# Taking the last 464 nodes of a graph layer as two groups of 232 instead of 384 and 80

## The chip, the cores and the metric

The kernel runs on one core of a Trainium2 chip. The metric is the time of one execution on the device in microseconds (us), lower is better, given as the median of several runs. The profile records one more execution of the same program.

## What is computed

A layer of a graph network with a residual and a layer norm, in float32, on 50,000 nodes of 128 features and 25,000 edges that are sorted by their target:

```
msg = relu(x[src] + edge_attr)            # 25000 x 128
agg = segment_sum(msg, dst, 50000)        # sum of the messages of each target node
h   = x + agg
h   = relu(relu(h @ W1 + b1) @ W2 + b2)   # 128 -> 256 -> 128
out = layernorm(x + h)                    # over the 128 features, no gain or bias
```

## The kernel before

**Groups and tiles.** The nodes are taken in groups of G = 384, three tiles (T = 3) of 128 nodes. Node `g*384 + 3*p + t` lies on partition p in tile t, so that the load or store of a group is one DMA with 128 partitions of 1,536 contiguous bytes. 50,000 nodes are 130 groups of 384 and one of 80 (LP = 80 partitions, LT = 1 tile). The last group has number 130 (`LAST`), the one before it 129 (`END`).

**Edges.** A group takes its messages from K = 2 chunks of 128 edges. Where a group's first chunk starts is found on the chip (`prepare`), from the sorted targets, and flags are set where the chunks would not hold all edges of a group; a slow general path stands behind them for such inputs. For each chunk `select` (L616) makes a matrix of zeros and ones, edge by node column, and the messages are multiplied with it on TensorE. An ordinary group's chunk reaches only 72 columns of each tile (WP), from column 0 or from column 56 (LO). The chunks of END reach 72 and 96 columns (END_WP), those of LAST all of its 80; LAST takes only one chunk, the last 128 edges.

**The steps of one group,** each with its engine:
- SyncE (SP) issues the load of x (`start_x`, L122), of the edge attributes (`start_edge_attr`, L126) and the store of the result (`store`, L552). GpSimd (POOL) issues the gathers x[src], one for each chunk (`start_gather`, L132).
- VectorE (DVE) adds the gathered rows to the edge attributes (`add_edge_attr`, L639). ScalarE (ACT) takes the relu as msg_hi (`high_part`, L809), and DVE the remainder msg_lo (`low_part`, L651).
- TensorE (PE) turns x into hT_ps (`turn_x` L906, or within `sum_turned` L934) and adds the messages there (`sum_messages` L916): hi and lo part of each chunk. ACT copies the sum (`copy_hT`, L815).
- PE makes the two halves of the hidden layer (`hidden_sum`, L973), ACT their relu (`hidden`, L821), PE the output (`output_sum`, L985).
- DVE adds b2 (`add_bias`, L658; for LAST a matmul with a row of ones does that, `bias_sum` L98), takes the relu and adds x (`add_x`, L674), and makes the statistics (`statistics` L686, `aggregate` L693). ACT makes the standard deviation (`deviation`, L827), DVE its reciprocal and the shift (`reciprocal` L702, `shifts` L707).
- The normalized result y is written by ACT (`normalize`, L837; tiles 0 and 1 of a group) and POOL (`third_tile`, L586; tile 2).

**What sets the order.** Each engine works through a list that is written out by hand (`main_sync`, `main_gpsimd`, `main_vector`, `main_scalar`, `main_tensor`), and semaphores hold an engine until its inputs are there. PE runs `hidden_sum(g)`, then the sum of the messages of g+1, then `output_sum(g)`. Loads are issued five groups ahead, gathers four.

**The end.** The last four groups have their tiles shared out one by one: POOL takes tiles 0 and 1 of group 127 and tiles 1 and 2 of END (L607), ACT tile 2 of group 127, all three of group 128 and tile 0 of END (L893 to L903), DVE the one tile of LAST (`normal_tile`, L713). The lines of the DVE's end are these:

```python
        add_x(LAST)
        statistics(LAST)
        reciprocal(END)
        shifts(END)
        aggregate(LAST)
        reciprocal(LAST)
        shifts(LAST)
        normal_tile(LAST, 0).then_inc(last_y_ready, 1)
```

SP then issues the store of END (L563) and of LAST (L583), 192 KB and 40 KB, and waits until all stores have landed.

Of the kernel before, what the change touches and what calls it, by code (L numbers as in the profile page):

```python
# [5 lines left out]
FP32R = mybir.dt.float32r  # L6
# [18 lines left out]
WP = 72  # L25
END_LO, END_WP = 32, 96
BOUNDS = [0, T * SPLIT, G]


FIRST_ROW = 2  # L30
LP, LT = 80, 1

# [21 lines left out]


def partitions(g, c):
    return LP if g == c["LAST"] else 128


def tiles(g, c):  # L60
    return LT if g == c["LAST"] else T


def windows(g, c):
    return 1 if g == c["LAST"] else K


def parts(g, c):

    return PARTS.get(g, [slice(0, windows(g, c))])  # L70

# [11 lines left out]
def gathers_to(slot, g, c):  # L83

    return 16 * sum(windows(i, c) for i in range(slot, g + 1, EB) if i >= FIRST_GROUPS)

# [39 lines left out]
def start_edge_attr(sp, edge_attr, g, first, c):  # L126
    n = windows(g, c)
    sp.dma_start(c["pre_msg"][:, g % EB, 0:n, :],
                 edge_attr[bass.ds(first, n * EW), :].rearrange("(k p) d -> p k d", p=EW)).then_inc(c["ea_loaded"][g % EB], 16)


def start_gather(nc, x, g, k, loaded, c):  # L132
    index = c["last_pairs"][:, 0:1] if g == c["LAST"] else c["src_of"][:, g - FIRST_ROW, k:k + 1]
# [28 lines left out]
def target_nodes(nc, dve, dst_ps, c):  # L162
    R = c["R"]
    base = c["node_row"][:, 0, :]
    dve.wait_ge(c["dst_T_ready"], 1)
    nc.vector.tensor_tensor(c["dst_of"][:, :, 0], dst_ps[:, 0, :], base, ALU.subtract)
    nc.vector.scalar_tensor_tensor(c["dst_of"][:, 0:R - 1, 1], dst_ps[:, 1, 0:R - 1], -float(T * LO[1]), base[:, 0:R - 1],
                                   ALU.add, ALU.subtract)
    return nc.vector.scalar_tensor_tensor(c["dst_of"][:, R - 1:R, 1], dst_ps[:, 1, R - 1:R], -float(T * END_LO), base[:, R - 1:R],
                                          ALU.add, ALU.subtract)  # L170
# [11 lines left out]
def prepare(nc, x, edge_attr, dst, pairs, w1, b1, w2, b2, c, sb, sem):  # L182
# [89 lines left out]
    def prepare_gpsimd(pool):  # L272
# [30 lines left out]
                       channel_multiplier=0, allow_small_or_imprecise_dtypes=True).then_inc(pool_consts, 1)  # L303
        nc.gpsimd.iota(c["node_in_last"][:, :], pattern=[[1, LP]], base=0,
                       channel_multiplier=0, allow_small_or_imprecise_dtypes=True).then_inc(pool_consts, 1)

# [87 lines left out]
    def prepare_vector(dve):  # L394
# [13 lines left out]
        for k in range(1, K + 1):  # L408
            last = nc.vector.tensor_scalar(node_row[:, k, :], node_row[:, k, :], float(BOUNDS[k]), None, ALU.add)
        link(dve, last)  # L410
        dve.wait_ge(pool_consts, 3)
        for k in range(1, K + 1):
            last = nc.vector.tensor_scalar(range_node[:, k:k + 1], range_node[:, k:k + 1], float(BOUNDS[k]), None, ALU.add)
        link(dve, last)
        nc.vector.tensor_scalar(least[:, :], range_node[:, K:K + 1], c["LAST"] * G - 0.5, float(edges - 2 * EW), ALU.is_gt, ALU.mult)

# [60 lines left out]
def main_path(nc, x, pairs, edge_attr, out, c, sb, sem, checks):  # L477
# [18 lines left out]

    x_src, sel, end_sel, last_sel = c["x_src"], c["sel"], c["end_sel"], c["last_sel"]
    msg_hi = sb("msg_hi", [128, EB, K, D], FP32R)
# [41 lines left out]
    def main_sync(sp):  # L540
# [5 lines left out]
        def load_ea(g):  # L546
            first = c["EDGES"] - EW if g == LAST else window_start_of(nc, g, c)
            if g >= EB:
                sp.wait_ge(msg_lo_ready, parts_to(g - EB + 1, c))
            start_edge_attr(sp, edge_attr, g, first, c)  # L550

        def store(g):  # L552
            if g < LAST - 3:
                sp.wait_ge(y_ready, g + 1)
                if g >= POOL_FROM:
                    sp.wait_ge(y_tile_ready, g - POOL_FROM + 1)
            elif g == LAST - 3:
                sp.wait_ge(y_pool_ready, 1)
            elif g == END:
                sp.wait_ge(y_pool_ready, 2)  # L560
            if g >= LAST - 3:
# [20 lines left out]
        sp.wait_ge(last_y_ready, 1)  # L582
        sp.dma_start(rows(out, LAST, c), y[0:LP, LAST % YB, 0:LT, :]).then_inc(out_stored[LAST % YB], 16)  # L583

    def main_gpsimd(pool):
# [8 lines left out]
        for g in range(FIRST_GROUPS, GROUPS):  # L594
# [3 lines left out]
            if g == LAST:  # L598
                pool.wait_ge(c["last_pairs_loaded"], 16)
            for k in range(windows(g, c)):  # L600
                start_gather(nc, x, g, k, xsrc_loaded[g % EB], c)
# [4 lines left out]

        for g, ts in ((LAST - 3, (0, 1)), (END, (1, 2))):  # L607
            pool.wait_ge(shift_ready, g + 1)
            pool.wait_ge(out_stored[g % YB], (g // YB) * 16)
            for t in ts:  # L610
                last = nc.gpsimd.tensor_scalar(y[:, g % YB, t, :], z[:, g % ZB, t, :], rstd[:, g % SB, t:t + 1],
                                               shift[:, g % SB, t:t + 1], ALU.mult, ALU.add)
# [190 lines left out]
    def main_scalar(act):  # L803
# [66 lines left out]
        for g in range(3, LAST):  # L870
# [6 lines left out]
            for t in range(T):  # L877
# [4 lines left out]
                if t == 0 and g == LAST_DST_AT:  # L882
                    act.wait_ge(c["last_pairs_loaded"], 16)
                    nc.scalar.activation(c["last_dst"][:, :], c["last_pairs"][:, 1:2], ACT.Copy).then_inc(last_dst_ready, 1)
                if t == 0 and g == END:
# [11 lines left out]
        normalize(LAST - 2, 0)  # L897
        normalize(LAST - 2, 1)
        normalize(LAST - 2, 2).then_inc(y_act_ready, 1)
        deviation(END)  # L900
        deviation(LAST)
        y_free(END)
        normalize(END, 0).then_inc(y_act_ready, 1)  # L903

    def main_tensor(pe):
# [10 lines left out]
        def sum_messages(g):  # L916

            n = tiles(g, c)
            pe.wait_ge(msg_lo_ready, parts_to(g, c) + 1)
            for k in range(windows(g, c)):  # L920
                if g == LAST:
                    p0, p1, tile = 0, LP, last_sel[:, :]
                elif g == END:
                    p0, p1 = (0, WP) if k == 0 else (END_LO, END_LO + END_WP)
                    tile = end_sel[:, k, :]
                else:
                    p0, p1, tile = LO[k], LO[k] + WP, sel[:, g % EB, k, :]
                cols = tile.rearrange("p (t q) -> p t q", t=n)[:, :, 0:p1 - p0]
                for part in (msg_hi, msg_lo):
                    last = nc.tensor.matmul(sum_bank(g)[:, 0:n, p0:p1], part[:, g % EB, k, :], cols,  # L930
                                            start=False, stop=(k == windows(g, c) - 1), skip_group_check=True)
            last.then_inc(hT_summed, 1)
# [331 lines left out]
def gnn_resnorm_kernel(nc, x, dst, pairs, edge_attr, w1, b1, w2, b2, out, h_dram):  # L1264
# [4 lines left out]
    GROUPS = -(-nodes // G)  # L1269
    assert D == 128 and HC * 128 == hidden and nodes == (GROUPS - 1) * G + LP * LT  # L1270
    R = GROUPS - 1 - FIRST_ROW

    ctx = ExitStack()
    with ctx:
# [6 lines left out]
        def sem(name):  # L1281
# [13 lines left out]
            node_in_range=sb("node_in_range", [128, 1, T * WP]),  # L1295
            node_in_last=sb("node_in_last", [128, LP]),
# [4 lines left out]
            last_pairs=sb("last_pairs", [EW, 2], INT32),  # L1301
            last_dst=sb("last_dst", [EW, 1]),
            last_pairs_loaded=sem("last_pairs_loaded"),
            end_sel=sb("end_sel", [EW, K, T * END_WP], FP32R),
            last_sel=sb("last_sel", [EW, LP], FP32R),
            first_sel=sb("first_sel", [EW, len(FIRST_SELS), T * 128], FP32R),
# [109 lines left out]
```

## Time and profile before

| | |
|---|---|
| median of 3 runs | 462.42 us (461.7 to 462.5) |
| the profiled execution: its time | 461.7 us |
| its span in the profile | 460.0 us |
| mean granted TensorE clock | 0.997 |
| PE, DVE, ACT, POOL busy | 98%, 94%, 86%, 80% |
| moved by DMA | 86.8 MB, 189 GB/s |

The time is what a run reports; the span is what the profiler recorded between the first and the last event of the same execution. A matmul on float32 is two records in the profile, so two matmuls stand there as x4. The ends of PE's records are modelled, so the distance from start to start says more than the duration. Names are those of the program with numbers left out: `h_ps` is h2_ps0 and h2_ps1, `w_sb` w1_sb and w2_sb, and so on. SPq is the queue in which SP issues DMAs. In a view of the DMA the line "DMA" gives the busy share of the 16 engines in tenths, in 40 equal slices of the stretch; "under 512 B" counts the small packets among all; a queue's line gives packets, MB, and the time that its packets took as a share of the 16 engines' time.

### The profile page before, as it was taken

The numbers are of one execution on the slowest core, as the hardware profiler recorded it, in microseconds if no ns is written. First come the engines' busy times: TensorE is split into PE (matmuls) and PEld (weight loads), VectorE is DVE, ScalarE is ACT, GpSimd is POOL, SyncE is SP. The second block draws the span as 40 slices with busy tenths as digits, with TensorE's granted clock in tenths as the row PEclk, the third lists the DMA queues.
The fourth block names the chain that finished last, engine by engine and source line by source line (L and its number), as shares of the span: only waits on it lengthen the run. The fifth ranks groups of instructions, "written<-read, shape, count | busy, mean of one in ns | idle before, by whom it ended". The sixth has DMA issues, their size and how long they took to land.

```text
span 460.0 us, 10662 instructions
## 1 busy us (share of the span) xinstructions
PE 451.1 (98%) x3033; PEld 379.3 (82%) x3033; DVE 433.6 (94%) x1759; ACT 394.2 (86%) x928; POOL 369.8 (80%) x403
## 2 busy tenths in 40 slices
PE   7999999999999999999999999999999999999995
PEld 6788888888888888888888888888888888888884
DVE  6799999999999999999999999999999999999996
ACT  3599888888888888988988888888888888888886
POOL 7777888888888888768888888888888888888842
PEclk9999999999999999999999999999999999999998
DMA  5576666666666666666666666666666666666632
GB/s 135 150 224 196 197 202 192 197 190 195 204 185 201 191 195 201 182 195 200 193 206 182 200 199 195 184 198 199 200 195 191 194 200 198 194 199 189 200 113 89
DMA packets 83870, 86.82 MB, mean 189 GB/s; under 512 B 12023, under 2 KB 79508, under 8 KB 83812
## 3 DMA queue, kind: packets, MB, share of 16 engines
q1 hardware_dynamic: 75044, 68.77, 48.0%
q0 software_dynamic: 8496, 17.38, 13.9%
q8 instruction: 24, 0.39, 0.4%
q14 instruction: 34, 0.28, 0.2%
q10 hardware_dynamic: 272, 0.00, 0.0%
HBM read 60.51 MB, written 25.60 MB: 187 GB/s over the span
## 4 chain that ended last, share of the span: by engine, by line
PE 95%; DMA 2%; DVE 1%; ACT 1%; issue 0%; DVEq 0%
PE h_ps L990 38%; PE h1T_ps L982 36%; PE hT_ps L942 11%; PE hT_ps L937 9%; DMA x_src<-in_x_dram,first_pairs 1%; DMA window<-in_pairs_dram,window_start_i 1%; DMA pre_msg<-in_edge_attr_dram 1%; DMA first_pairs<-in_pairs_dram 0%; DVE stats L690 0%; PE hT_ps L913 0%; PE hT_ps L930 0%; DVE pre_msg L648 0%; DVE z L683 0%; DVE before_in_row L321 0%; ACT std L830 0%
## 5 line engine op out<-in xcount | busy, mean ns | idle before, releaser
L134 POOL DMA_INDIRECT x_src<-in_x_dram,src_of x254 | 270.2, 1064 | 67.5 <-issue 59.8
L990 PE MATMUL h_ps<-w_sb,h1T 128*128 128x128 f32 x1564 | 198.0, 276 | 0.0
L982 PE MATMUL h1T_ps<-hT,w_sb 128*128 128x384 f32 (+1 forms) x524 | 190.2, 486 | 0.5 <-ACT hT L819 0.5
L990 PEld LDWEIGHTS h_ps<-w_sb,h1T 128*128 128x128 f32 x1564 | 185.3, 192 | 0.3 <-ACT h1T L825 0.2
L825 ACT ACTIVATE h1T<-h1T_ps,b_sb 128x384 f32<-128x384 f32 (+1 forms) x262 | 151.3, 578 | 37.6 <-PE h1T_ps L982 29.3
L982 PEld LDWEIGHTS h1T_ps<-hT,w_sb 128*128 128x128 f32 x524 | 89.5, 191 | 35.2 <-ACT hT L819 0.7
L844 ACT ACTIVATE y<-z,shift,rstd 128x128 f32<-128x128 f32 x263 | 114.6, 483 | 1.1 <-DVE shift L710 0.4
L590 POOL TENSOR_SCALAR y<-z,rstd,shift 128x128 f32<-128x128 f32 x123 | 87.4, 711 | 13.5 <-DVE shift L710 9.0
L942 PE MATMUL hT_ps<-sel,msg_hi 128*128 128x216 f32 x250 | 94.8, 447 | 0.0
L690 DVE BATCH_NORM_STATS2 stats<-z 128x6 f32<-128x128 f32 x391 | 88.6, 282 | 0.1
L937 PE MATMUL hT_ps<-ident,x_sb 128*128 128x128 f32 x375 | 87.6, 273 | 0.0
L664 DVE TENSOR_TENSOR h<-h_ps,b_sb 128x384 f32<-128x384 f32 x130 | 72.3, 556 | 15.1 <-PE h_ps L990 2.1
L631 DVE TENSOR_TENSOR sel<-node_in_range,dst_of 128x432 fp32r<-128x432 f32 x126 | 76.0, 603 | 0.0
L683 DVE SCALAR_TENSOR_TENSOR z<-h,x_sb 128x384 f32<-128x384 f32 x130 | 71.8, 552 | 0.0
L942 PE MATMUL hT_ps<-sel,msg_lo 128*128 128x216 f32 x250 | 70.1, 348 | 0.0
L813 ACT ACTIVATE msg_hi<-pre_msg 128x256 fp32r<-128x256 f32 (+1 forms) x134 | 55.0, 411 | 15.0 <-DVE pre_msg L648 10.2
L819 ACT ACTIVATE hT<-hT_ps 128x384 f32<-128x384 f32 (+1 forms) x130 | 63.5, 488 | 3.3 <-PE hT_ps L968 2.4
L937 PEld LDWEIGHTS hT_ps<-ident,x_sb 128*128 128x128 f32 x375 | 53.0, 141 | 15.1
L942 PEld LDWEIGHTS hT_ps<-sel,msg_hi 128*128 128x128 f32 x250 | 47.4, 190 | 18.3 <-issue 3.9
L648 DVE TENSOR_TENSOR pre_msg<-pre_msg,x_src 128x256 f32<-128x256 f32 (+1 forms) x134 | 57.9, 432 | 3.2 <-DMA x_src<-in_x_dram,first_pairs 1.6
L655 DVE SCALAR_TENSOR_TENSOR msg_lo<-pre_msg,msg_hi 128x256 fp32r<-128x256 f32 (+1 forms) x134 | 55.1, 411 | 2.6 <-ACT msg_hi L813 1.2
L942 PEld LDWEIGHTS hT_ps<-sel,msg_lo 128*128 128x128 f32 x250 | 47.5, 190 | 0.1
(120 smaller groups left out, 183.3 us busy)
## 6 DMA issues: line engine op xcount, KB each, us to landing
x_sb<-in_x_dram SPq DMA_DIRECT2D x130, 192.0 KB, 2.5
out_dram<-y SPq DMA_DIRECT2D x130, 192.0 KB
pre_msg<-in_edge_attr_dram SPq DMA_DIRECT2D x130, 128.0 KB, 2.8
x_src<-in_x_dram,src_of POOLq DMA_INDIRECT x254, 3.0
w_sb<-in_w_dram SPq DMA_DIRECT2D x2, 128.0 KB, 2.6
dst_rows<-in_dst_dram SPq DMA_DIRECT2D x1, 97.7 KB
x_src<-in_x_dram,first_pairs POOLq DMA_INDIRECT x6, 2.8
b_sb<-in_b_dram SPq DMA_DIRECT2D x1, 64.0 KB, 3.2
```

The costliest lines, as they stand in the source:

```text
L134: nc.gpsimd.indirect_dma_start(out=c["x_src"][:, g % EB, k, :], out_offset=None, in_=x, in_offset=bass.IndirectOffsetOnAxis(ap=index, axis ...
L590: nc.gpsimd.tensor_scalar(y[:, g % YB, 2, :], z[:, g % ZB, 2, :], rstd[:, g % SB, 2:3], shift[:, g % SB, 2:3], ALU.mult, ALU.add).then_inc ...
L631: nc.vector.tensor_tensor(sel[:, g % EB, :, :], node_in_range[:, :, :].to_broadcast([128, K, T * WP]), dst_of[:, g - FIRST_ROW:g - FIRST_R ...
L664: nc.vector.tensor_tensor(h2[0:p, g % 2, 0:n, :], h2_ps[g % 2][0:p, 0:n, :], b2_sb[0:p, :, :].to_broadcast([p, n, D]), ALU.add).then_inc(h ...
L683: nc.vector.scalar_tensor_tensor(z[0:p, g % ZB, 0:n, :], h2_of[0:p, 0:n, :], 0.0, x_sb[0:p, g % XB, 0:n, :], ALU.max, ALU.add).then_inc(z_ ...
L690: last = nc.vector.bn_stats(stats[0:p, g % SB, t, :], z[0:p, g % ZB, t, :])
L825: nc.scalar.activation(h1T[:, h, 0:n, 0:p], h1T_ps[h][:, 0:n, 0:p], ACT.Relu, bias=b1_sb[:, h:h + 1]).then_inc(h1_ready, 1)
L844: return nc.scalar.activation(y[0:p, g % YB, t, :], z[0:p, g % ZB, t, :], ACT.Identity, bias=shift[0:p, g % SB, t:t + 1], scale=rstd[0:p, ...
L937: nc.tensor.matmul(hT_ps[:, t, :], x_sb[:, g % XB, t, :], ident[:, :], is_transpose=True, start=False, stop=False, skip_group_check=True)
L942: return nc.tensor.matmul(hT_ps[:, 0:T, LO[k]:LO[k] + WP], part[:, g % EB, k, :], cols, start=start, stop=stop, skip_group_check=True)
L982: nc.tensor.matmul(h1T_ps[h][:, 0:n, 0:p], w1_sb[:, h * 128:(h + 1) * 128], hT[:, 0:n, 0:p], start=True, stop=True).then_inc(h1_summed, 1)
L990: last = nc.tensor.matmul(h2_ps[g % 2][0:p, t, :], h1T[:, h, t, 0:p], w2_sb[:, h, :], start=(h == 0 and t == 0 and not biased(g, c)), stop ...
```

## The change

The number of groups stays 131. The groups 129 (END) and 130 (LAST) become halves of the last 464 nodes: 116 partitions (HALF_P) and two tiles (HALF_T), 232 nodes each. Both take two chunks of edges, and every chunk's matrix reaches all 232 columns (`half_sel`, `node_in_half` take the place of `end_sel`, `last_sel`, `node_in_last`). The chunks of LAST are the last 256 edges. The bounds that `prepare` looks for are capped at the first node of LAST. The tiles at the end are shared out anew: POOL takes tiles 0 and 1 of group 127, tile 2 of group 128 and tile 1 of END; ACT tile 2 of 127, tiles 0 and 1 of 128, tile 0 of END and tile 1 of LAST; DVE tile 0 of LAST. The core of the diff:

```diff
-END_LO, END_WP = 32, 96
-LP, LT = 80, 1
+HALF_P, HALF_T = 116, 2
+HALF = HALF_P * HALF_T
...
+def half(g, c):
+    return g >= c["LAST"] - 1
 def partitions(g, c):
-    return LP if g == c["LAST"] else 128
+    return HALF_P if half(g, c) else 128
 def tiles(g, c):
-    return LT if g == c["LAST"] else T
+    return HALF_T if half(g, c) else T
+def first_node(g, c):
+    return (c["LAST"] - 1) * G + HALF if g == c["LAST"] else g * G
...
 def rows(dram, g, c):
-    t = tiles(g, c)
-    return dram[g * G:g * G + partitions(g, c) * t, :].rearrange("(p t) d -> p t d", t=t)
+    t, n0 = tiles(g, c), first_node(g, c)
+    return dram[n0:n0 + partitions(g, c) * t, :].rearrange("(p t) d -> p t d", t=t)
...
-            sp.dma_start(rows(out, g, c), y[:, g % YB, :, :]).then_inc(out_stored[g % YB], 16)
+            sp.dma_start(rows(out, g, c), y[0:partitions(g, c), g % YB, 0:tiles(g, c), :]).then_inc(out_stored[g % YB], 16)
...
-        sp.dma_start(c["last_pairs"][:, :], pairs[c["EDGES"] - EW:c["EDGES"], :]).then_inc(c["last_pairs_loaded"], 16)
+        sp.dma_start(c["last_pairs"][:, :, :], pairs[c["EDGES"] - K * EW:c["EDGES"], :].rearrange("(k p) a -> p k a", p=EW),
+                     allow_slow_non_contiguous=True).then_inc(c["last_pairs_loaded"], 16)
...
         sp.wait_ge(last_y_ready, 1)
-        sp.dma_start(rows(out, LAST, c), y[0:LP, LAST % YB, 0:LT, :]).then_inc(out_stored[LAST % YB], 16)
+        sp.wait_ge(y_act_ready, 4)
+        sp.dma_start(rows(out, LAST, c), y[0:HALF_P, LAST % YB, 0:HALF_T, :]).then_inc(out_stored[LAST % YB], 16)
...
-        for g, ts in ((LAST - 3, (0, 1)), (END, (1, 2))):
+        for g, ts in ((LAST - 3, (0, 1)), (LAST - 2, (2,)), (END, (1,))):
...
-                for k, width in ((0, WP), (1, END_WP)):
-                    last = nc.vector.tensor_scalar(
-                        end_sel[:, k, :].rearrange("p (t q) -> p t q", t=T)[:, :, 0:width],
-                        c["node_in_group"][:, :].rearrange("p (t q) -> p t q", t=T)[:, :, 0:width],
-                        dst_of[:, g - FIRST_ROW, k:k + 1], None, ALU.is_equal)
-                last.then_inc(sel_ready, 1)
+                nc.vector.tensor_tensor(half_sel[:, 0, :, :], c["node_in_half"][:, :, :].to_broadcast([128, K, HALF]),
+                                        dst_of[:, g - FIRST_ROW:g - FIRST_ROW + 1, :].rearrange("p a k -> p k a").to_broadcast([128, K, HALF]),
+                                        ALU.is_equal).then_inc(sel_ready, 1)
...
-                nc.vector.tensor_scalar(last_sel[:, :], c["node_in_last"][:, :], c["last_dst"][:, 0:1], -float(LAST * G),
-                                        ALU.subtract, ALU.is_equal).then_inc(sel_ready, 1)
+                for k in range(K):
+                    last = nc.vector.tensor_scalar(half_sel[:, 1, k, :], c["node_in_half"][:, 0, :], c["last_dst"][:, k:k + 1],
+                                                   -float(first_node(LAST, c)), ALU.subtract, ALU.is_equal)
+                last.then_inc(sel_ready, 1)
...
         normalize(LAST - 2, 0)
-        normalize(LAST - 2, 1)
-        normalize(LAST - 2, 2).then_inc(y_act_ready, 1)
+        normalize(LAST - 2, 1).then_inc(y_act_ready, 1)
         deviation(END)
-        deviation(LAST)
         y_free(END)
         normalize(END, 0).then_inc(y_act_ready, 1)
+        deviation(LAST)
+        act.wait_ge(shift_ready, LAST + 1)
+        y_free(LAST)
+        normalize(LAST, 1).then_inc(y_act_ready, 1)
```

How the lists of the engines change is shown at two places.

The end of ScalarE's list before, from the hidden layer of LAST on (std is a `deviation`, y a `normalize`):

```order
L825 ACTIVATE h1T<-h1T_ps1,b1_sb 128x80 [waits h1_summed]
L844 ACTIVATE y<-z,shift,rstd 128x128 [waits shift_ready,out_stored1]
L844 ACTIVATE y<-z,shift,rstd 128x128 [waits shift_ready,out_stored2]
L844 ACTIVATE y<-z,shift,rstd 128x128 x2
L830 ACTIVATE std<-mean_var,eps_col 128x3 [waits var_ready]
L830 ACTIVATE std<-mean_var,eps_col 80x1 [waits var_ready]
L844 ACTIVATE y<-z,shift,rstd 128x128 [waits shift_ready,out_stored3]
```

The same with the change:

```order
L832 ACTIVATE h1T<-h1T_ps1,b1_sb 128x2x116 [waits h1_summed]
L851 ACTIVATE y<-z,shift,rstd 128x128 [waits shift_ready,out_stored1]
L851 ACTIVATE y<-z,shift,rstd 128x128 [waits shift_ready,out_stored2]
L851 ACTIVATE y<-z,shift,rstd 128x128
L837 ACTIVATE std<-mean_var,eps_col 116x2 [waits var_ready]
L851 ACTIVATE y<-z,shift,rstd 116x128 [waits shift_ready,out_stored3]
L837 ACTIVATE std<-mean_var,eps_col 116x2 [waits var_ready]
L851 ACTIVATE y<-z,shift,rstd 116x128 [waits out_stored4,shift_ready]
```

One `normalize` of group 128 has left the list, the one of END now stands ahead of the `deviation` of LAST, and a `normalize` of LAST has come at the end.

The end of SyncE's list before, the last loads and the stores:

```order
L563 DMA out_dram<-y 128x384 [waits y_tile_ready,y_ready]
L123 DMA x_sb<-in_x_dram 80x128 [waits z_ready]
L128 DMA pre_msg<-in_edge_attr_dram 128x128 [waits msg_lo_ready]
L563 DMA out_dram<-y 128x384 [waits y_tile_ready,y_ready] x6
L563 DMA out_dram<-y 128x384 [waits y_act_ready,y_pool_ready]
L563 DMA out_dram<-y 128x384 [waits y_act_ready]
L563 DMA out_dram<-y 128x384 [waits y_act_ready,y_pool_ready]
L583 DMA out_dram<-y 80x128 [waits last_y_ready]
```

The same with the change:

```order
L568 DMA out_dram<-y 128x384 [waits y_tile_ready,y_ready]
L129 DMA x_sb<-in_x_dram 116x256 [waits z_ready]
L133 DMA pre_msg<-in_edge_attr_dram 128x2x128 [waits msg_lo_ready]
L568 DMA out_dram<-y 128x384 [waits y_tile_ready,y_ready] x6
L568 DMA out_dram<-y 128x384 [waits y_act_ready,y_pool_ready] x2
L568 DMA out_dram<-y 116x256 [waits y_act_ready,y_pool_ready]
L590 DMA out_dram<-y 116x256 [waits y_act_ready,last_y_ready]
```

The count of DMAs is the same; the last two stores have 116 partitions of 1,024 bytes each, in place of 128 partitions of 1,536 and 80 of 512.

## Rows read from the trace of the kernel before

**Rows 1.** The page: span, and the chain that ended last.

```profile
span 460.0 us, 10662 instructions
...
PE 95%; DMA 2%; DVE 1%; ACT 1%; issue 0%; DVEq 0%
```

**Rows 2.** Timeline of PE, 449 to 453 us: start, duration, line, operation.

```profile
451.00 0.28 PE L930 MATMUL hT_ps<-last_sel,msg_hi 128*128 128x80 f32 x1
...
451.22 1.58 PE L990 MATMUL h_ps<-w_sb,h1T 128*128 128x128 f32 x12
452.64 0.57 PE L982 MATMUL h1T_ps<-hT,w_sb 128*128 128x80 f32 x4
```

**Rows 3.** Chain that ended last, in order of time, 452 to 460 us.

```profile
452.44 0.19 ACT std L830
...
452.87 0.21 DVE shift L710
453.07 0.48 DVE h L664
...
453.57 0.57 DVE z L683
...
454.17 0.69 DVE stats L690 x3
...
454.98 0.31 DVE mean_var L699 x3
...
455.50 0.29 DVE stats L690
...
455.90 0.17 DVE shift L710
...
456.18 0.30 ACT std L830
...
456.89 0.34 DVE y L717
```

**Rows 4.** Timeline of all engines, 455.9 to 457.6 us.

```profile
456.16 0.88 POOL L611 TENSOR_SCALAR y<-z,rstd,shift 128x128 f32<-128x128 f32 x2 [2.67 <-DVE shift L710]
...
456.38 0.48 ACT L844 ACTIVATE y<-z,shift,rstd 128x128 f32<-128x128 f32 x1
...
457.06 0.33 SPq L563 DMA_DIRECT2D out_dram<-y  x1
...
457.45 0.42 SPq L583 DMA_DIRECT2D out_dram<-y  x1
```

**Rows 5.** DMA, 457.2 to 460 us: the stores of END and LAST.

```profile
DMA  0000000000799999997762000000000000000000
...
DMA packets 240, 0.24 MB, mean 85 GB/s; under 512 B 32, under 2 KB 240, under 8 KB 240
```

**Rows 6.** DMA, 455.9 to 456.8 us: the store of group 128 alone.

```profile
DMA packets 144, 0.20 MB, mean 219 GB/s; under 512 B 16, under 2 KB 144, under 8 KB 144
...
q1 hardware_dynamic: 144, 0.20, 60.0%
```

**Rows 7.** DMA, 0 to 3 us: the first loads of the targets.

```profile
DMA packets 558, 0.02 MB, mean 8 GB/s; under 512 B 530, under 2 KB 558, under 8 KB 558
...
q10 hardware_dynamic: 272, 0.00, 4.8%
```

**Rows 8.** DMA, 2.9 to 3.2 us: the load of dst_rows alone.

```profile
q1 hardware_dynamic: 29, 0.02, 26.1%
```

**Rows 9.** Groups by line and form, 440 to 460 us: busy us, mean ns, idle.

```profile
L655 DVE SCALAR_TENSOR_TENSOR msg_lo<-pre_msg,msg_hi 128x256 fp32r<-128x256 f32 x3 | 1.3, 418 | 0.0
...
L683 DVE SCALAR_TENSOR_TENSOR z<-h_ps,x_sb 80x128 f32<-80x128 f32 x1 | 0.3, 254 | 0.0
```

**Rows 10.** Timeline of SP and POOL, 437 to 441 us: last load of x, last gather.

```profile
437.68 0.33 SPq L123 DMA_DIRECT2D x_sb<-in_x_dram  x1
...
439.43 0.98 POOL L134 DMA_INDIRECT x_src<-in_x_dram,last_pairs  x1 [0.17 <-issue]
```

More of the change, by code:

```diff
@@ L53 @@
 FLAGS = 7 + FIRST_CHUNKS + UPPER_CHUNKS
+def half(g, c):
+    return g >= c["LAST"] - 1
 def partitions(g, c):
-    return LP if g == c["LAST"] else 128
+    return HALF_P if half(g, c) else 128
 def tiles(g, c):
-    return LT if g == c["LAST"] else T
-def windows(g, c):
-    return 1 if g == c["LAST"] else K
+    return HALF_T if half(g, c) else T
+def first_node(g, c):
+    return (c["LAST"] - 1) * G + HALF if g == c["LAST"] else g * G
 def parts(g, c):
-    return PARTS.get(g, [slice(0, windows(g, c))])
+    return PARTS.get(g, [slice(0, K)])
 def parts_to(g, c):
@@ L83, in gathers_to @@
 def gathers_to(slot, g, c):
-    return 16 * sum(windows(i, c) for i in range(slot, g + 1, EB) if i >= FIRST_GROUPS)
+    return 16 * K * len([i for i in range(slot, g + 1, EB) if i >= FIRST_GROUPS])
 def biased(g, c):
@@ L126, in start_edge_attr @@
 def start_edge_attr(sp, edge_attr, g, first, c):
-    n = windows(g, c)
-    sp.dma_start(c["pre_msg"][:, g % EB, 0:n, :],
-                 edge_attr[bass.ds(first, n * EW), :].rearrange("(k p) d -> p k d", p=EW)).then_inc(c["ea_loaded"][g % EB], 16)
+    sp.dma_start(c["pre_msg"][:, g % EB, :, :],
+                 edge_attr[bass.ds(first, K * EW), :].rearrange("(k p) d -> p k d", p=EW)).then_inc(c["ea_loaded"][g % EB], 16)
 def start_gather(nc, x, g, k, loaded, c):
-    index = c["last_pairs"][:, 0:1] if g == c["LAST"] else c["src_of"][:, g - FIRST_ROW, k:k + 1]
+    index = c["last_pairs"][:, k, 0:1] if g == c["LAST"] else c["src_of"][:, g - FIRST_ROW, k:k + 1]
     nc.gpsimd.indirect_dma_start(
@@ L303, in prepare_gpsimd @@
                        channel_multiplier=0, allow_small_or_imprecise_dtypes=True).then_inc(pool_consts, 1)
-        nc.gpsimd.iota(c["node_in_last"][:, :], pattern=[[1, LP]], base=0,
-                       channel_multiplier=0, allow_small_or_imprecise_dtypes=True).then_inc(pool_consts, 1)
+        nc.gpsimd.iota(c["node_in_half"][:, 0, :].rearrange("p (t q) -> p t q", t=HALF_T), pattern=[[1, HALF_T], [HALF_T, HALF_P]],
+                       base=0, channel_multiplier=0, allow_small_or_imprecise_dtypes=True).then_inc(pool_consts, 1)
     chain = [0]
@@ L408, in prepare_vector @@
         for k in range(1, K + 1):
-            last = nc.vector.tensor_scalar(node_row[:, k, :], node_row[:, k, :], float(BOUNDS[k]), None, ALU.add)
+            last = nc.vector.tensor_scalar(node_row[:, k, :], node_row[:, k, :], float(BOUNDS[k]),
+                                           float(first_node(c["LAST"], c)), ALU.add, ALU.min)
         link(dve, last)
@@ L412, in prepare_vector @@
         for k in range(1, K + 1):
-            last = nc.vector.tensor_scalar(range_node[:, k:k + 1], range_node[:, k:k + 1], float(BOUNDS[k]), None, ALU.add)
+            last = nc.vector.tensor_scalar(range_node[:, k:k + 1], range_node[:, k:k + 1], float(BOUNDS[k]),
+                                           float(first_node(c["LAST"], c)), ALU.add, ALU.min)
         link(dve, last)
-        nc.vector.tensor_scalar(least[:, :], range_node[:, K:K + 1], c["LAST"] * G - 0.5, float(edges - 2 * EW), ALU.is_gt, ALU.mult)
+        nc.vector.tensor_scalar(least[:, :], range_node[:, K:K + 1], first_node(c["LAST"], c) - 0.5, float(edges - (K + 1) * EW),
+                                ALU.is_gt, ALU.mult)
         dve.wait_ge(first_loaded, 16)
@@ L546, in load_ea @@
         def load_ea(g):
-            first = c["EDGES"] - EW if g == LAST else window_start_of(nc, g, c)
+            first = c["EDGES"] - K * EW if g == LAST else window_start_of(nc, g, c)
             if g >= EB:
@@ L556, in store @@
                     sp.wait_ge(y_tile_ready, g - POOL_FROM + 1)
[L557 to L561, printed above, removed]
+            else:
+                sp.wait_ge(y_pool_ready, g - (LAST - 3) + 1)
                 sp.wait_ge(y_act_ready, g - (LAST - 3) + 1)
-            sp.dma_start(rows(out, g, c), y[:, g % YB, :, :]).then_inc(out_stored[g % YB], 16)
+            sp.dma_start(rows(out, g, c), y[0:partitions(g, c), g % YB, 0:tiles(g, c), :]).then_inc(out_stored[g % YB], 16)
         sp.wait_ge(c["starts_row_ready"], 1)
@@ L599, in main_gpsimd @@
                 pool.wait_ge(c["last_pairs_loaded"], 16)
-            for k in range(windows(g, c)):
+            for k in range(K):
                 start_gather(nc, x, g, k, xsrc_loaded[g % EB], c)
@@ L605, in main_gpsimd @@
             third_tile(g)
-        for g, ts in ((LAST - 3, (0, 1)), (END, (1, 2))):
+        for g, ts in ((LAST - 3, (0, 1)), (LAST - 2, (2,)), (END, (1,))):
+            p = partitions(g, c)
             pool.wait_ge(shift_ready, g + 1)
@@ L610, in main_gpsimd @@
             for t in ts:
-                last = nc.gpsimd.tensor_scalar(y[:, g % YB, t, :], z[:, g % ZB, t, :], rstd[:, g % SB, t:t + 1],
-                                               shift[:, g % SB, t:t + 1], ALU.mult, ALU.add)
+                last = nc.gpsimd.tensor_scalar(y[0:p, g % YB, t, :], z[0:p, g % ZB, t, :], rstd[0:p, g % SB, t:t + 1],
+                                               shift[0:p, g % SB, t:t + 1], ALU.mult, ALU.add)
             last.then_inc(y_pool_ready, 1)
@@ L627, in select @@
                 dve.wait_ge(c["pool_consts"], 9)
-                nc.vector.tensor_scalar(last_sel[:, :], c["node_in_last"][:, :], c["last_dst"][:, 0:1], -float(LAST * G),
-                                        ALU.subtract, ALU.is_equal).then_inc(sel_ready, 1)
+                for k in range(K):
+                    last = nc.vector.tensor_scalar(half_sel[:, 1, k, :], c["node_in_half"][:, 0, :], c["last_dst"][:, k:k + 1],
+                                                   -float(first_node(LAST, c)), ALU.subtract, ALU.is_equal)
+                last.then_inc(sel_ready, 1)
             else:
@@ L883, in main_scalar @@
                     act.wait_ge(c["last_pairs_loaded"], 16)
-                    nc.scalar.activation(c["last_dst"][:, :], c["last_pairs"][:, 1:2], ACT.Copy).then_inc(last_dst_ready, 1)
+                    nc.scalar.activation(c["last_dst"][:, :], c["last_pairs"][:, :, 1], ACT.Copy).then_inc(last_dst_ready, 1)
                 if t == 0 and g == END:
@@ L919, in sum_messages @@
             pe.wait_ge(msg_lo_ready, parts_to(g, c) + 1)
[L920 to L925, printed above, removed]
+            for k in range(K):
+                if half(g, c):
+                    p0, p1, tile = 0, HALF_P, half_sel[:, g - END, k, :]
                 else:
@@ L930, in sum_messages @@
                     last = nc.tensor.matmul(sum_bank(g)[:, 0:n, p0:p1], part[:, g % EB, k, :], cols,
-                                            start=False, stop=(k == windows(g, c) - 1), skip_group_check=True)
+                                            start=False, stop=(k == K - 1), skip_group_check=True)
             last.then_inc(hT_summed, 1)
@@ L1269, in gnn_resnorm_kernel @@
     GROUPS = -(-nodes // G)
-    assert D == 128 and HC * 128 == hidden and nodes == (GROUPS - 1) * G + LP * LT
+    assert D == 128 and HC * 128 == hidden and nodes == (GROUPS - 2) * G + 2 * HALF
     R = GROUPS - 1 - FIRST_ROW
@@ L1300, in gnn_resnorm_kernel @@
             first_dst=sb("first_dst", [EW, FIRST_CHUNKS]),
-            last_pairs=sb("last_pairs", [EW, 2], INT32),
-            last_dst=sb("last_dst", [EW, 1]),
+            last_pairs=sb("last_pairs", [EW, K, 2], INT32),
+            last_dst=sb("last_dst", [EW, K]),
             last_pairs_loaded=sem("last_pairs_loaded"),
-            end_sel=sb("end_sel", [EW, K, T * END_WP], FP32R),
-            last_sel=sb("last_sel", [EW, LP], FP32R),
+            half_sel=sb("half_sel", [EW, 2, K, HALF], FP32R),
             first_sel=sb("first_sel", [EW, len(FIRST_SELS), T * 128], FP32R),
```

6 lines of the change are left out of this document (3 added, 3 removed).

## The prediction

> **What bounds the kernel now.** I read the page first: the chain that ended last is 95% TensorE [rows 1]. Over nearly the whole span the time is PE's, and the change touches the work of PE only in the last two of 131 groups. So I went to the end: the timeline of PE, then the chain in order of time, then what SP issues, then the DMA.
>
> PE's output for END starts at 451.22 and the hidden layer of LAST at 452.64 [rows 2]. From there PE does not set the end any more. The chain runs through a deviation on ACT at 452.44 (group 128) to the DVE, which makes the shift of group 128 at 452.87 and only then comes to END: bias (h) 453.07, z 453.57, three statistics 454.17, three aggregates 454.98; then LAST: z, statistics 455.50; shift of END 455.90; deviation of LAST on ACT 456.18; the last y on the DVE, 456.89 + 0.34 = 457.23 [rows 3]. SP issues the store of END at 457.06 and that of LAST at 457.45 [rows 4]. Their bytes move from slice 9 to slice 21 of 0.07 us, so from 457.84 to 458.74 [rows 5]. From the last byte to the end of the span, 460.0, pass 1.26 us. From issue (457.06) to the first byte are 0.78 us.
>
> **PE, part by part.** The hidden layer and the output do the same work in all: 464 columns, and 3 + 1 = 2 + 2 tiles. The sums of messages grow: 6 matmuls become 8, each of 232 columns. LAST's stood 0.11 us apart (two from 451.00 to 451.22) [rows 2], so LAST's two additional ones and its second tile of x cost some 0.3 us. On the other side, END's output, 1.42 us from 451.22 to 452.64, shrinks by a third and its hidden layer by about as much, 0.9 us together. LAST's messages now have 256 elements per partition on the DVE, 0.42 us [rows 9], and its selection takes two operations, so they are ready later; I allow PE a wait of 0.1 us for it, with bounds of 0 and 0.5. Sum for PE at 452.64: about 0.5 us earlier. It is worth nothing, because the DVE's list has the reciprocal and shift of group 128 ahead of END's bias, and those hang on ACT's deviation at 452.44, which hangs on full groups. END's bias stays at 453.05.
>
> **The DVE's and ACT's end.** An operation on 128 elements takes 0.25 us, on 384 about 0.56, one on 256 about 0.42 [rows 3, 9]. END: bias -0.14, z -0.14, one statistic fewer -0.20, one aggregate fewer -0.08. LAST: z +0.17, one statistic +0.20, one aggregate +0.08. So END's shift comes at 455.76 and LAST's variance at 456.08, near what they were. New is ACT's order: `normalize` of END starts at 455.98 when END's shift is there, and the `deviation` of LAST stands behind it. A `normalize` is 0.48 long [rows 4], and the next operation may start a little before its end: 456.40, where it was 456.18. From deviation to y were 0.71 us [rows 3], so the two tiles of LAST start at 457.11. ACT's tile takes 0.48, not the DVE's 0.34: 457.59. SP, which waited until it had issued END's store, is free now, and issues LAST's at 457.61, 0.16 us later than before. END's store goes earlier: POOL has one tile of it instead of two, half of the 0.88 us [rows 4], so it is issued at 456.52 and moves its first byte at 457.32.
>
> **The stores.** Here I expect the loss. The store of a full group alone is 144 packets, 16 of them small, for 128 partitions [rows 6]. So a store has one packet of data for a partition and, it seems, one small packet for each DMA engine that it runs on. The last two agree: 240 packets are 128 + 80 and 32 small ones, 16 for each store [rows 5]. The first loads of the targets are another matter: before 3 us there were 530 - 272 = 258 small packets on SP's queue [rows 7]. Two loads of 4-byte elements with 125 and 124 partitions give 249. That leaves 9, not 32. 125 = 5 x 25 and 124 = 4 x 31: 5 + 4 engines, when the partitions have to fall into equal shares on up to 16 engines. The load with 125 partitions says the same: 26.1% of 16 is 4.2 engines busy [rows 8]. 128 and 80 divide by 16; **116 = 4 x 29 does not.** By this both new stores run on 4 engines.
>
> How long is a packet of 1,024 bytes on one engine? The full store took 60.0% of 16 x 0.9 us [rows 6], 8.64 us of engine time, for 128 packets of 1,536 bytes: 67.5 ns each at most, 45 scaled by bytes. The load of 800-byte packets took 0.261 x 16 x 0.3 = 1.25 us for 29: 43 ns each, 55 scaled [rows 8]. I take 48 ns, between the two and nearer to the store; the bounds are 43 and 67.5. A store of 29 packets on an engine then takes 1.39 us (1.25 to 1.96). Both stores sit on the same engines if these are always the same ones, and queue: END 457.32 to 458.71. LAST could begin at 457.61 + 0.78 = 458.39, waits until 458.71 and ends at 460.10. Before, the last byte was at 458.74: **+1.36 us**, from 459.82 (+1.1) to 461.24 (+2.5).
>
> [...]
>
> **What is hidden.** The loads of x for both groups run on 4 engines too, 1.4 us each, and what follows them in the queue may wait as long. The last is issued at 437.68 and its group turned after 450 [rows 10, 2]: over 8 us to spare; without that cover a late x would move PE one for one, 1 us. The second gather of LAST adds about 1.25 us to POOL at 439.43 [rows 10], and POOL is idle for 2.67 us before its last pair [rows 4]. The wider iota, the doubled last_pairs load near 23 us and the cap in `prepare` change an element count or an operand of instructions off the chain: nothing, up to 0.1 us.
>
> **Sum.** 461.7 us of the profiled execution + 1.4 = 463.1; it lies 0.7 below the median of the runs, so against 462.42 the forecast is **463.8 us**.
>
> **Rivals.**
> - *The stores spread over 16 engines after all* (uneven shares, or another way for stores; the 9 small packets are only of loads). Then LAST's 116 KB take some 0.45 us: 458.39 to 458.84, +0.1 us: 462.5. For it: no store here has a partition count that 16 does not divide. Against it: [rows 7, 8]. The chance is 0.12.
> - *Four engines, but each faster than in [rows 6],* where 16 share the way to memory. At a fifth less than the 45 ns, some 36, a store takes 1.0 us, LAST runs 458.39 to 459.4: +0.7, 463.1. Against it: 4 to 5 engines alone took 43 ns for less data [rows 8]. Chance 0.15.
> - *Faster:* PE's half microsecond counts. This needs the deviation of group 128 off ACT's path: if ACT, whose copies and relus of END have shrunk by a third, comes to it 0.4 us earlier, and the DVE too, the end moves by as much. It decides only where the DVE's list of group 128 is shorter, and it is longer by 0.3 us (LAST's selection and messages). With 16 engines this gives 462.42 + 0.1 - 0.6 = 461.9, within 0.2%; to pass that limit PE and the DVE would both have to gain over 1 us. Chance of that 0.03.
> - *Slower by more:* the two stores at the upper bound, or a load on 4 engines that holds up END's edge attributes: 464.9. Chance 0.08.
> - The change may not do what it says: if the flags sent the work to the general path, the time would be far above any here. A group of 232 nodes has about 116 edges and two chunks hold 256; under 0.01.
>
> **How the numbers follow.** About 0.2%, 0.92 us, is what a measurement can tell from no change. The forecast case (+1.1 to +1.7) has 0.62 and is slower, the upper one 0.08 too; of the faster-engine case I count a fifth as slower. Slower 0.73, same 0.24, faster 0.03. The range goes from 462.5 (spread stores) to 464.8 (a packet near 60 ns).
>
> **What would show it.** The DMA between 457 and 461 us with 8 small packets instead of 32 for the last two stores and a busy share near a quarter (2 tenths) over some 2.8 us; the last y at 457.6 by ACT; END's store issued before 456.7. I am wrong if the last two stores show 32 small packets and 9 tenths, if bytes end before 459, or if the time changed already in the full groups ahead of 446 us.

## The result and the profile after

| | before | the change |
|---|---|---|
| median | 462.32 us (461.7 to 462.5, 6 runs) | 463.99 us (463.72 to 464.32, 6 runs) |
| ratio, 95% interval | | 1.0039 (1.0026 to 1.0052) |
| span in the profile | 460.0 us | 462.3 us |

The change makes the kernel slower: by 1.67 us between the medians, by 0.39% in the ratio, which is taken over all runs. The forecast was 463.8 us, slower, with a range from 462.5 to 464.8.

First the question whether the full groups took part. The timeline of PE shows where the hidden layer of group 128 begins, before:

```profile
446.23 0.81 PE L982 MATMUL h1T_ps<-hT,w_sb 128*128 128x384 f32 x2
```

and with the change:

```profile
446.05 0.81 PE L988 MATMUL h1T_ps<-hT,w_sb 128*128 128x384 f32 x2
```

At 446 us the profiled execution of the change is even 0.18 us ahead: 0.06 us of that stand after 24 us, the rest comes in small steps over the full groups, none of it from the last two groups. The span is 2.3 us longer, so 2.5 us were lost in the last 16 us. The mean granted clock, 0.993 against 0.997, is no cause: it is 1.00 in both profiles from 440 to 456 us, while PE still multiplies, and is lower only behind PE's last work, 0.81 before and 0.55 with the change from 456 to 458 us. The chain that ended last in the change, from the output of END on (start, length, what):

```profile
451.20 0.87 PE h_ps L996 x8
452.07 0.79 PE h1T_ps L988 x4
452.86 0.61 PE h_ps L109 x2
...
453.61 1.07 PE h_ps L996 x8
...
454.70 0.43 DVE z L690
...
455.75 0.17 DVE shift L717
...
456.41 0.29 ACT std L837
...
457.12 0.49 ACT y L851
```

PE comes to the hidden layer of LAST at 452.07, where it was 452.64 [rows 2]. END's shift is at 455.75 (455.90 before), LAST's deviation at 456.41 (456.18), the last y at 457.12 + 0.49 = 457.61 (457.23) [rows 3]. So the engines' work ends 0.38 us later. From the timeline of SP and ACT, the two last stores:

```profile
456.57 0.28 SPq L568 DMA_DIRECT2D out_dram<-y  x1
...
457.68 0.28 SPq L590 DMA_DIRECT2D out_dram<-y  x1
```

END's is issued 0.49 us earlier than before, LAST's 0.23 later [rows 4]. The rest lies behind them. The DMA from 457 to 462.3 us in the kernel before, busy tenths and GB/s in slices of 0.1325 us:

```profile
DMA  0000002999975000000000000000000000000000
GB/s 0 0 0 0 0 0 81 336 371 371 325 166 143 0 0 0 0 0 0 0 0 0 0 0 0 0 0 0 0 0 0 0 0 0 0 0 0 0 0 0
```

and in the change:

```profile
DMA  0002222122222122213131221100000000000000
GB/s 0 0 31 70 46 70 85 54 93 93 100 93 93 46 77 54 62 46 62 54 85 62 100 93 70 46 23 23 23 23 15 0 0 0 0 0 0 0 0 0
DMA packets 240, 0.24 MB, mean 45 GB/s; under 512 B 8, under 2 KB 240, under 8 KB 240
...
q1 hardware_dynamic: 240, 0.24, 14.7%
```

The same 0.24 MB that went at up to 371 GB/s within 0.9 us before now take 3.8 us: mostly 46 to 100 GB/s, 23 and less in the last 0.7 us, with two tenths of the 16 engines busy, and 8 small packets where there were 32 [rows 5]. The last byte moves at about 461.1 instead of 458.7, and the span ends 1.2 us behind it, as before.

### The profile page after: what moved, and what is told of

It is laid out like the page before. It is cut to its first block, busy times and chain, and to the rows that moved or that the text cites. A ratio compares the mean times of both kernels' runs of the same rounds, so it can differ in the third digit from the quotient of the medians.

```text
span 462.3 us, 10671 instructions
## 1 busy us (share of the span) xinstructions
PE 451.1 (98%) x3035; PEld 379.5 (82%) x3035; DVE 433.9 (94%) x1759; ACT 394.4 (85%) x928; POOL 370.6 (80%) x404
## 3 DMA queue, kind: packets, MB, share of 16 engines
q1 hardware_dynamic: 75300, 68.83, 48.1%
## 4 chain that ended last, share of the span: by engine, by line
PE 95%; DMA 2%; SPq 0%; POOL 0%; DVE 0%; issue 0%; ACT 0%; ACTq 0%
PE h_ps L996 38%; PE h1T_ps L988 36%; PE hT_ps L948 11%; PE hT_ps L943 9%; DMA window<-in_pairs_dram,window_start_i 1%; DMA first_pairs<-in_pairs_dram 1%; DMA pre_msg<-in_edge_attr_dram 0%; POOL x_src L153 0%; PE hT_ps L936 0%; PE hT_ps L922 0%; PE h_ps L109 0%; ACT y L851 0%; PE hT_ps L974 0%; PE hT_ps L969 0%; DVE stats L697 0%
## 5 line engine op out<-in xcount | busy, mean ns | idle before, releaser
L996 PE MATMUL h_ps<-w_sb,h1T 128*128 128x128 f32 (+1 forms) x1564 | 197.9, 276 | 0.0
L996 PEld LDWEIGHTS h_ps<-w_sb,h1T 128*128 128x128 f32 (+1 forms) x1564 | 185.4, 192 | 0.3 <-ACT h1T L832 0.2
L671 DVE TENSOR_TENSOR h<-h_ps,b_sb 128x384 f32<-128x384 f32 (+1 forms) x130 | 72.1, 554 | 15.0 <-PE h_ps L996 1.5
L690 DVE SCALAR_TENSOR_TENSOR z<-h,x_sb 128x384 f32<-128x384 f32 (+1 forms) x130 | 71.5, 550 | 0.0
```

The costliest lines, as they stand in the source:

```text
L671: nc.vector.tensor_tensor(h2[0:p, g % 2, 0:n, :], h2_ps[g % 2][0:p, 0:n, :], b2_sb[0:p, :, :].to_broadcast([p, n, D]), ALU.add).then_inc(h ...
L690: nc.vector.scalar_tensor_tensor(z[0:p, g % ZB, 0:n, :], h2_of[0:p, 0:n, :], 0.0, x_sb[0:p, g % XB, 0:n, :], ALU.max, ALU.add).then_inc(z_ ...
L996: last = nc.tensor.matmul(h2_ps[g % 2][0:p, t, :], h1T[:, h, t, 0:p], w2_sb[:, h, :], start=(h == 0 and t == 0 and not biased(g, c)), stop ...
```

## The experiments

The runs stand in three sets, each with the kernel before timed beside it; what counts is the excess over that median. It is 461.94 us in the first set (the cuts of both stores and of the last one, ACT's queue, 116 and 12), 461.91 in the second (112 and 16, 240 and 224 nodes, the deviation first, the loads), 461.81 in the third (END's store cut, END's tile 0 by the DVE, the change once more). Theory 1 is that of the forecast: a DMA whose partitions 16 does not divide runs on few engines. The stores are cut by a small helper:

```python
def store_pieces(sp, out, y, g, cuts, c):
    for p0, p1 in cuts:
        sp.dma_start(rows(out, g, c)[p0:p1, :, :], y[p0:p1, g % YB, 0:tiles(g, c), :]).then_inc(c["out_stored"][g % YB], 16)
```

**Both last stores cut into 112 and 4 partitions.**

```diff
-            sp.dma_start(rows(out, g, c), y[0:partitions(g, c), g % YB, 0:tiles(g, c), :]).then_inc(out_stored[g % YB], 16)
+            store_pieces(sp, out, y, g, [(0, 112), (112, 116)] if g == END else [(0, 128)], c)
...
-        sp.dma_start(rows(out, LAST, c), y[0:HALF_P, LAST % YB, 0:HALF_T, :]).then_inc(out_stored[LAST % YB], 16)
+        store_pieces(sp, out, y, LAST, [(0, 112), (112, 116)], c)
```

> Theory 1 (few DMA engines): a store of 116 partitions runs on 4 engines; cut into 112 and 4 partitions the large piece runs on 16 (7 packets each). Then the last two stores show 16 + 4 small packets each, 40 in all instead of 8, the last byte lands at about 458.9 instead of 461.1 us, and the time falls by 2.1 us against the change, to 461.9 to 462.2, level with before. Theory 2 (the packets of 1,024 bytes or the row addresses are slow, however many engines): the packets are the same, nothing changes but one more issue for each store, time as the change (464.0) or 0.3 above. Theory 3 (the order of the engines at the end lost it): as the change, too.

Measured: 462.82 us, 0.88 over before (ratio 1.0018, 1.0009 to 1.0027). The DMA from 457 to 462.3 us:

```profile
DMA  0059851000379620000000000000000000000000
...
DMA packets 272, 0.24 MB, mean 45 GB/s; under 512 B 40, under 2 KB 272, under 8 KB 272
```

Two short bursts up to 9 tenths, 40 small packets as expected, the last byte at 459.1. The same bytes in the same packets of 1,024 and the same work of the engines: against the change's 2.19 us over before in the third set, 1.3 us are gone, and theories 2 and 3, by which nothing would be gained, can hold at most for the rest. The time is 0.6 us above the range expected, though; the runs below take that up.

**Only the last store cut.**

> Only the last store is cut into 112 and 4 partitions, END's stays whole on few engines. Theory 1: END's store still occupies engines 0 to 3 until about 459.2; the pieces of the last one on the other 12 engines are done by then, those on engines 0 to 3 wait behind it and end near 459.6: time about 1.5 us below the change, 462.5, and 0.5 above both cut. Theory 2: as the change.

Measured: 462.97 us, 1.03 over before (1.0012 to 1.003), 0.5 above the expected 462.5; last byte at 459.5. The last byte is 0.4 us later than with both cut, as expected, but the time only 0.15, because with both cut the span ended 1.6 us behind the last byte and here 1.4. That the engines would be those with the numbers 0 to 3 is not shown: the trace gives no numbers of the engines, only how many are busy, two tenths of 16 while END's store runs alone.

**Only END's store cut.**

> The change with only END's store cut into 112 and 4 partitions; the last store stays whole on 4 engines. Theory 1: END's bytes are gone by 458.1, the last store finds its engines free, its 29 packets on each take 1.5 to 2.0 us from 458.4: last byte 460.0 to 460.4, against 461.1 with both whole. Time 463.0 to 463.4. With the run that cuts only the last one (462.97) this parts the loss into the last store's own length (about 1.2) and the queue behind END's (0.7 to 0.9). A rival, that only the last store's own length matters, gives 464.0 again.

Measured: 463.23 us, 1.42 over before (1.002 to 1.0041). Its DMA shows the parts one after the other, first END's burst, then the last store alone on its few engines:

```profile
DMA  0001697300002222122222000000000000000000
GB/s 0 0 0 46 201 255 248 116 31 0 0 31 70 46 77 77 62 100 93 93 100 85 31 23 8 0 0 0 0 0 0 0 0 0 0 0 0 0 0 0
```

The last store alone moves from 458.5 to 460.3, 1.8 us. So of the change's late end (461.1 against 458.7) 0.8 us are the queue behind END's store (461.1 against 460.3; the time agrees, 1.42 over before instead of 2.19). The other 1.6 us are the last store itself: issued 0.3 us later than before's, and 1.8 us long where both stores together took 0.9.

**The last store issued by ACT's queue.**

```diff
         normalize(LAST, 1).then_inc(y_act_ready, 1)
+        act.wait_ge(last_y_ready, 1)
+        act.wait_ge(y_act_ready, 4)
+        act.dma_start(rows(out, LAST, c), y[0:HALF_P, LAST % YB, 0:HALF_T, :]).then_inc(out_stored[LAST % YB], 16)
```

> The last store (116 partitions, whole) is issued by ACT's queue instead of SP's, at about the same time. If the two stores queue up behind each other in SP's queue, another queue lets them run side by side on other engines: last byte near 459.7, 1.4 us less than the change. If they queue because both use the same 4 engines (theory 1), packets of the two alternate there, and the last byte comes at the same time as in the change, within 0.3 us: 464.0.

Measured: 464.83 us, 2.89 over before (1.0043 to 1.007). The DMA from 457 to 462.3 us (its first slice still belongs to the store of group 128):

```profile
DMA  2000000000222122222212211313222110000000
...
q1 hardware_dynamic: 139, 0.13, 7.9%
q10 hardware_dynamic: 120, 0.12, 7.3%
```

The bytes come from two queues now, and still no slice shows more than 3 tenths; from the first byte of END's store to the last of all are again 3.8 us (458.2 to 462.0). Two stores on four engines each, if they were not the same four, would show up to 5 tenths; so both queues feed the same four engines. The 0.8 us by which the time missed the expectation were there long before the end. The same relu of an early group's hidden layer, in this kernel

```profile
25.54 0.58 ACT L829 ACTIVATE h1T<-h1T_ps,b_sb 128x384 f32<-128x384 f32 x1
```

and in the change

```profile
24.64 0.58 ACT L832 ACTIVATE h1T<-h1T_ps,b_sb 128x384 f32<-128x384 f32 x1
```

stand 0.9 us apart. The start was slower in this program: a wait of the DVE for loaded rows (`add_edge_attr`) ends at 15.07 us where it ended at 14.21 in the change. Why they were late stays open.

**The kernel before with END's store cut into 116 and 12 partitions.** The same helper with `[(0, 116), (116, 128)]`, in the kernel before.

> The kernel before, with the store of END (128 partitions of 1,536 bytes) cut into 116 and 12 partitions; nothing else changed. Theory 1: 116 run on 4 engines with 29 packets of 1,536 bytes each, some 2.0 to 2.6 us from 457.84, so until about 460.1, and the small last store behind it: 1.4 us or more slower than before, 463.7 to 464.4, with 4 + 12 + 16 = 32 small packets and a quarter of the engines busy. Theories 2 and 3: as before plus at most the one more issue of 0.3 us, 462.3 to 462.6.

Measured: 463.80 us, 1.86 over before (1.0025 to 1.0052). The DMA from 457 to 462.3 us:

```profile
DMA  0000000229283423444544222100000000000000
...
DMA packets 240, 0.24 MB, mean 45 GB/s; under 512 B 32, under 2 KB 240, under 8 KB 240
```

One number, 116, put into the kernel before makes it about as slow as the whole change. 32 small packets are 4 + 12 + 16; with 16 engines for each of the three DMAs they would be 48.

**Its control, 112 and 16 partitions.**

> Control for the cut into 116 and 12: the kernel before with END's store cut into 112 and 16 partitions, both on 16 engines by theory 1: 48 small packets, a second issue of 0.33 us that pushes the last store back by as much. Time 462.2 to 462.4, 0.3 to 0.4 us above before and 1.5 below the cut at 116. If the cut as such cost the 1.9 us, it shows here too: 463.8.

Measured: 462.25 us, 0.34 over before (0.9997 to 1.0015, an interval that holds zero):

```profile
DMA  0000000169996316400000000000000000000000
...
DMA packets 256, 0.24 MB, mean 45 GB/s; under 512 B 48, under 2 KB 256, under 8 KB 256
```

The 48 small packets and 9 tenths are back. So a second issue costs some 0.3 us here at most, and the number 116 the other 1.5.

**240 and 224 nodes.** 120 and 112 partitions of two tiles:

```diff
-HALF_P, HALF_T = 116, 2
-HALF = HALF_P * HALF_T
+HALF_P, HALF_T = (120, 112), 2
+HALF = HALF_P[0] * HALF_T
...
-    return HALF_P if half(g, c) else 128
+    return HALF_P[g - c["LAST"] + 1] if half(g, c) else 128
```

> The change with halves of 240 and 224 nodes (120 and 112 partitions of two tiles) in place of 232 and 232; whole stores, one issue each. Theory 1 in the form of equal shares (the largest number up to 16 that divides the partitions): END's store on 15 engines, LAST's on 16, 31 small packets in all; last byte near 458.9 and no additional issue on SP, 0.4 us below the kernel with both stores cut: 462.0 to 462.4 where before has 461.9. If instead anything that 16 does not divide falls to 4 engines, END's shows 4 small packets and the time is near the one with only the last store cut. If the packets of 1,024 bytes are slow (theory 2): as the change, 463.6 and more.

Measured: 462.52 us, 0.61 over before (1.0004 to 1.0022):

```profile
DMA  0000688930002897200000000000000000000000
...
DMA packets 263, 0.24 MB, mean 45 GB/s; under 512 B 31, under 2 KB 263, under 8 KB 263
...
q1 hardware_dynamic: 263, 0.24, 16.6%
```

31 small packets are 15 + 16. It is not that all which 16 does not divide falls to 4 engines: 120 partitions take 15. With theory 1 in the form of equal shares 4, 15 and 16 engines for 116, 120 and 112 partitions agree: 8 small packets for the change's two stores of 116, 31 here. Against both stores cut this is 0.27 us less (0.88 to 0.61, in different sets), about the price of an additional issue; the time is 0.1 us above the range expected.

**The same with the deviation of LAST first.**

```diff
+        deviation(LAST)
         y_free(END)
         normalize(END, 0).then_inc(y_act_ready, 1)
-        deviation(LAST)
```

> As the one with 240 and 224, and on ACT the deviation of LAST ahead of the normalize of END. The normalize of END is then ready first but waits for LAST's variance, 0.1 us later; LAST's last tiles start 0.2 us earlier, as the prediction priced the order. Expected 0.1 to 0.25 us below the one with 240 and 224, within 0.1% of before. A rival: END's store, now later, lies in front of LAST's, and nothing is gained.

Measured: 462.16 us, 0.25 over before (0.9994 to 1.0013), 0.36 below the run above. ACT's deviation of LAST starts at 456.18 in this profile, and the last store is issued at 457.47:

```profile
456.18 0.29 ACT L837 ACTIVATE std<-mean_var,eps_col 112x2 f32<-112x2 f32 x1 [1.16 <-DVE mean_var L706]
456.38 1.02 ACT L851 ACTIVATE y<-z,shift,rstd 120x128 f32<-120x128 f32 x2
...
457.47 0.33 SPq L590 DMA_DIRECT2D out_dram<-y  x1
```

**And END's tile 0 by the DVE.**

```diff
         aggregate(LAST)
+        normal_tile(END, 0).then_inc(y_end_ready, 1)
         reciprocal(LAST)
```

> 240 and 224 nodes with the deviation of LAST first, and END's tile 0 normalized by the DVE, in the 0.35 us in which it waits for that deviation, instead of by ACT. END's store is issued 0.3 to 0.4 us earlier (456.6), its bytes no longer run beside those of the last store; the last y may come 0.05 later. By the theory that the end hangs on the last issue and the bytes behind it: 0 to 0.15 us below the kernel without this, 462.0 to 462.2, level with before. If more than 0.3 us comes off, END's bytes were in the way of the last ones even on 16 engines.

Measured: 462.14 us, 0.33 over before (0.9999 to 1.0017). END's store is issued at 456.59 instead of 456.93, and nothing is gained (462.16 us without it): on 15 engines END's bytes are not in the way.

**The loads of x cut, the stores whole.**

> The change with its two loads of x cut into 112 and 4 partitions, the stores left whole. By the prediction the loads on 4 engines are hidden (over 10 us ahead of their use): as the change, 1.0036 to 1.0042 of before, PE's work on the last groups at the same places. If they held up the edge attributes or x of the last groups, the time falls by up to 1 us.

Measured: 464.11 us, 2.20 over before (1.0033 to 1.006), last byte near 461.2 (461.1 in the change). The whole run has 32 packets more on SP's queue than the change, 75,332 against 75,300: 16 + 4 small ones for each load of x where the whole load has 4. So the change's loads run on four engines, and that is hidden.

**The change once more.**

> The change once more, unaltered, on the same chip as its variants, to have them against one another: 1.0036 to 1.0042 of before, 463.6 to 464.0.

Measured: 464.00 us, 2.19 over before (1.003 to 1.0057), with 14.7% of the engines' time from 457 to 462.3 us as in the first profile. The median is the one of the first measurement within 0.01 us; it is before's that came out 0.4 to 0.5 us lower in the three sets, over 18 to 27 runs instead of 6.

## Why the prediction was right

**What bounds the end, and where PE's gain goes.** Right. PE reaches the hidden layer of LAST 0.57 us earlier, 0.4 when its 0.18 us of lead at 446 are taken off, where 0.5 was forecast, and END's bias starts at 452.80, 0.2 us earlier than before's 453.00. That is no more than the lead: the wait for the shift of group 128 kept the rest. One detail was missed. With 256 columns in the matmul of the bias and eight records of output, PE is in the chain once more: LAST's z starts at 454.70, when PE's output ends (453.61 + 1.07), where I had the DVE alone set it. It is worth 0.1 us, since the DVE's operation before it ends at 454.58.

**The order on ACT.** Right, to 0.02 us: deviation of LAST at 456.41 against 456.40 forecast, y at 457.12 against 457.11. That the agreement is so close is in part luck: this execution was 0.18 us ahead in the full groups, so against them each of these times, and the two issues below, is up to 0.2 us later than forecast. (The operations listed for the DVE also add up to 455.71 for END's shift, not to 455.76.) Taking the order away in the kernel with 240 and 224 nodes gave 0.36 us, more than the 0.2 of the forecast.

**The issues.** END's store at 456.57 (456.52), LAST's at 457.68 (457.61).

**The stores.** The mechanism was right, the term too small. I took 48 ns a packet from the two nearest rows. The profile of the change has 14.7% of 16 x 5.3 us: 12.5 us, which is 54 ns for each of the 232 packets of data, and 3.1 us on each of four engines, where I had 2.8. The rest, some 0.7 us, no row of before could show: the four engines do not finish together. From 460.4 on one engine alone works, at 23 GB/s. The DMA of the change from 460.42 to 461.08 us has 6.6% of 16 engines, which is one:

```profile
DMA packets 16, 0.02 MB, mean 23 GB/s; under 512 B 1, under 2 KB 16, under 8 KB 16
...
q1 hardware_dynamic: 16, 0.02, 6.6%
```

So the last byte is at 461.1 and not at 460.1. The mean of 54 ns is no steady pace: at the 93 to 100 GB/s of the best slices four engines take 41 to 44 ns a packet, and the slices at 31 to 77 GB/s, many of them where a store begins, make up the difference.

**The queue.** Right: both stores share four engines, in one queue as in two, and the wait behind END's store is worth 0.8 us of the last byte.

**The sum.** The forecast was 1.4 us over before; measured were 1.67 and, in the third set, 2.19. The size was 0.3 to 0.8 short. The profiled executions differ by 2.3 us, 1.0 more than forecast, and that is the missing part of the stores. That 463.8 came within 0.2 us of 463.99 is therefore luck in part: the median of before that it starts from, 462.42, was 0.5 to 0.6 us above that of the later sets, and this made up for much of what the stores lacked. The upper end of the range was also put down to the wrong packet: 60 ns give 464.5 us, and 464.8 needs 66 ns.

**The rivals.** That the stores spread over 16 engines fell with 8 small packets; that four engines alone are faster per packet, some 36 ns, fell with a mean of 54 and 41 at best (that 16 share the way to memory no run shows by itself; the 232 packets of 240 and 224 nodes, on 15 and 16 engines, took 16.5% of 16 x 5.3 us, 60 ns each); PE's half microsecond did not reach the end; the general path was not taken.

**What is left.** With whole shares and the old order the 240 and 224 nodes stand 0.25 us over before, an interval that holds zero. The last store's issue, 457.47 against 457.45, does not explain that rest, but its size may: 112 KB stand behind that issue instead of 40, and the last byte is at 459.05 instead of 458.74, the span 460.3 instead of 460.0 us. No kernel here beats the one before: two groups of two tiles have the same four tiles at the end as three and one, and the work of PE that is saved does not lie on the path. Cutting both stores also left the span end 1.6 us behind the last byte instead of 1.2; why was not tried.

## What to carry to other kernels

When a tile gets a new number of partitions, ask of each of its DMAs into how many equal shares, at most 16, that number divides: here 116 ran on 4 engines, 120 on 15, 112 on 16. The loads of x on 4 engines, issued over 12 us ahead of their use, cost nothing (2.20 us over before with them cut, 2.19 whole); a store at the very end costs its whole length, here 1.8 us on 4 engines, and two in a row queued on the same four, 0.8 us more. The small packets in these traces, 16 for a whole store of 128 partitions and 8 for two of 116, show this before a kernel is changed, even if only two odd loads at the start have such a shape.

## What the runs showed of the hardware that was not expected

- As the forecast's queue had it, but now shown: two DMAs of 116 partitions from two different queues did not run side by side: 3 tenths busy at most, 3.8 us for both, as from one queue. Another queue was no way around the four busy engines.
- Of four engines with equal shares one ended some 0.7 us after the others, at 23 GB/s alone, in both profiles of the change. With the last store alone on the four engines (END's store cut) only the last two slices, 0.3 us, are that slow: the lag was longer with two stores on them than with one. Why one engine lags was not tried.
- An issue on SP was shortest on 4 engines: 0.27 to 0.28 us for a whole store of 116 partitions in every profile, against 0.33 to 0.42 for the last stores on 16 engines and 0.39 on 15.
